# Eight-stage block on one core: dummy matmuls taken out of TensorE's queue, and sixteen of the value-output copies moved from ScalarE to VectorE

## The reference, cut to what is computed

```python
x = x + tanh(g_xattn[0]) * linear_attention(ctx, ctx, layernorm(x))      # stage 0
x = x + tanh(g_ffn[0])   * experts_top1(layernorm(x))                    # stage 1, 8 experts, GELU
x = x + tanh(g_xattn[1]) * normed_cross_attention(layernorm(x), ctx)     # stage 2
x = x + tanh(g_ffn[1])   * experts_top2_and_shared(layernorm(x))         # stage 3, 8 experts + 1, SiLU
x = x + tanh(g_xattn[2]) * causal_attention(layernorm(x), ctx, ctx)      # stage 4, 16 heads of 64
x = x + tanh(g_ffn[2])   * quantized_conv_mlp(layernorm(x))              # stage 5
x = x + tanh(g_xattn[3]) * attention_over_ctx_and_x(...)                 # stage 6, 16 heads
x = x + tanh(g_ffn[3])   * coupled_mlp(layernorm(x))                     # stage 7, 3 cycles
```

```python
x[t] += w1[t] * y1[t] + w2[t] * y2[t]       # "combine"
```

## Time and profile before

| | before |
|---|---|
| median of 3 runs | 2359.4 us (2356.04 to 2359.98) |
| the profiled execution | 2356.04 us |
| its span, first to last instruction | 2354.2 us |
| TensorE matmul busy | 2181.8 us, 93% of the span |
| VectorE busy | 1418.2 us, 60% |
| ScalarE busy | 988.6 us, 42% |
| GpSimd busy | 131.5 us, 6% |
| mean granted TensorE clock | 0.964 |

### The profile page before, as it was taken

The page is one execution under the profiler, slowest core; times in us unless marked ns, Lnnn a source line. Parts: engine busy times, 40 slices in busy tenths (PEclk is TensorE's granted clock), DMA queues, the critical chain, the costliest instruction groups (busy, mean ns, idle before and its releaser), DMA issues. The chain is left out here.

```text
span 2354.2 us, 33701 instructions
## 1 busy us (share of the span) xinstructions
PE 2181.8 (93%) x12946; PEld 1549.2 (66%) x12946; DVE 1418.2 (60%) x3011; ACT 988.6 (42%) x1829; POOL 131.5 (6%) x122
## 2 busy tenths in 40 slices
PE   7996999987999899797799999999999999999988
PEld 4874899444899778645566666666666666666643
DVE  5974111573344678787566666666666666666555
ACT  5222433431111422378444454444444445445345
POOL 1002011005122000000100000000000000000000
PEclk9996999988999999899899999999999999999999
DMA  3603897123699600200000000000000000000001
GB/s 115 171 1 110 278 326 274 55 76 108 200 326 320 209 1 1 77 1 1 11 1 1 1 1 1 1 1 1 1 1 1 1 1 1 1 1 1 1 0 36
DMA packets 109258, 159.73 MB, mean 68 GB/s; under 512 B 12555, under 2 KB 85165, under 8 KB 109101
## 3 DMA queue, kind: packets, MB, share of 16 engines
q1 hardware_dynamic: 101805, 134.80, 17.4%
q0 software_dynamic: 7296, 22.78, 3.0%
HBM read 127.64 MB, written 29.91 MB: 67 GB/s over the span
## 5 line engine op out<-in xcount | busy, mean ns | idle before, releaser
L595 PE MATMUL ps<-arena,w_odd 128*128 128x128 f32 (+4 forms) x2352 | 438.7, 440 | 3.1 <-DVE arena L1975 1.2
L595 PE MATMUL ps<-arena 128*64 128x256 f32 (+5 forms) x2852 | 411.0, 389 | 24.1 <-DVE arena L2058 7.5
L2272 DVE TENSOR_REDUCE small<-ps 128x1 f32<-128x1024 f32 x256 | 312.5, 1221 | 87.1 <-PE ps L595 87.1
L595 PEld LDWEIGHTS ps<-arena 128*64 128x64 f32 (+4 forms) x2852 | 266.9, 150 | 138.3 <-issue 31.3
L1590 ACT ACTIVATE arena<-ps 128x512 f32<-128x512 f32 x256 | 139.0, 595 | 453.0 <-PE ps L1090 452.9
L595 PEld LDWEIGHTS ps<-arena,w_odd 128*128 128x128 f32 (+3 forms) x2352 | 246.9, 188 | 106.5 <-issue 101.2
L1597 ACT ACTIVATE w_odd<-ps,small 128x1101 f32<-128x1101 f32 x256 | 302.5, 1182 | 10.2 <-DVE small L2273 8.5
L1090 PEld LDWEIGHTS ps<-ident,w_odd 128*128 128x128 f32 x2048 | 222.3, 140 | 121.2 <-issue 109.9
L1090 PE MATMUL ps<-ident,w_odd 128*128 128x128 f32 x2048 | 281.0, 277 | 9.8 <-DVE arena L2213 3.1
L2290 DVE COPY arena<-ps 128x512 f32<-128x512 f32 x256 | 164.3, 682 | 4.3 <-PE ps L1090 2.0
L595 PE MATMUL ps<-xn_feat,w_even 128*128 128x512 f32 (+1 forms) x352 | 138.5, 525 | 2.8 <-DVE xn_feat L1875 1.9
(11 more groups left out here) (360 smaller groups left out, 2855.9 us busy)
## 6 DMA issues: line engine op xcount, KB each, us to landing
w_odd<-in_s_w SPq DMA_DIRECT2D x32, 1024.0 KB, 6.9
w_odd<-in_s_wgu SPq DMA_DIRECT2D x30, 704.0 KB, 5.8
w_even<-in_s_w SPq DMA_DIRECT2D x15, 1024.0 KB, 7.2
arena<-expert_rows_in SPq DMA_DIRECT2D x62, 130.0 KB, 4.5
w_odd<-in_s_wd SPq DMA_DIRECT2D x30, 256.0 KB, 3.5
out_feat<-in_s_wgu SPq DMA_DIRECT2D x10, 704.0 KB, 5.6
expert_rows_in<-zero_row POOLq DMA_DIRECT2D x1, 5070.0 KB, 33.3
vo_rows<-w_odd SPq DMA_DIRECT2D x8, 616.0 KB
```

Source lines behind the costliest of these rows:

```text
L595: return pe.matmul(o, lhsT, rhs, start=start, stop=stop, **kw)
L2272: link(dve.tensor_reduce(m, s6_main[h], AX.X, ALU.max, negate=True))
```

## The change

Two things are edited. First, `keep_busy` and its calls are removed, 139 dummy matmuls in all (72 + 34 + 6 + 3 x 9). Second, of the 32 vo copies of stage 3's end the 16 with even u leave ScalarE. VectorE makes them, in a function `vo_copies4(g)` that `combine` calls after each of its four groups: after group g it copies the units 8g, 8g + 2, 8g + 4 and 8g + 6, each when its product is there. The counts of the semaphores follow: `mk_no` counts one mk copy per unit and one vo copy for every second, and `vo_copied` waits on `vo_sb` for an even unit and on `prep_sb` for an odd one.

```diff
--- before.py
+++ after.py
@@ -344,11 +344,14 @@
 
         def mk_no(u):
 
-            return KT + 8 + 2 * u + 1
+            return KT + 8 + u + 1 + u // 2
 
         def vo_copied(eng, u):
 
-            eng.wait_ge(prep_sb, KT + 8 + 2 * u + 2)
+            if u % 2 == 0:
+                eng.wait_ge(vo_sb, VT + 8 + u // 2 + 1)
+            else:
+                eng.wait_ge(prep_sb, KT + 8 + u + 1 + (u + 1) // 2)
 
         up_base = {1: 0, 3: E0 * NB if 1 in stages else 0}
         dn_base = {1: 0, 3: NT if 1 in stages else 0}
@@ -594,16 +597,9 @@
             def mm(o, lhsT, rhs, start=True, stop=True, **kw):
                 return pe.matmul(o, lhsT, rhs, start=start, stop=stop, **kw)
 
-            def keep_busy(bank, n):
-
-                for _ in range(n):
-                    mm(PS[:, bank, :], identb[:, :], identb[:, :].unsqueeze(1).broadcast_to([P, 4, P]))
-
             def layer_norm(s):
 
                 n, tr, half = ln_no[s], tr_no[s], half_no[s]
-                if s in (2, 3, 4):
-                    keep_busy(7, 9)
                 for g in range(4):
                     if g < 2:
                         pe.wait_ge(ln_xn, NT * xn_no[n] + 8 * g + 8)
@@ -878,7 +874,6 @@
                 pe.wait_ge(dn_add, NT)
                 expert_tiles(1)
                 context2()
-                keep_busy(0, 72)
 
             def stage3():
                 layer_norm(3)
@@ -921,7 +916,6 @@
                 pe.wait_ge(dn_add, dn_base[3] + NT)
                 expert_tiles(3)
                 context4()
-                keep_busy(0, 6)
 
             def context2():
 
@@ -961,7 +955,6 @@
                     if t < NT - 4:
                         pe.wait_ge(x2_x, t + 1)
                         rows_part(t + 4)
-                keep_busy(3, 34)
 
             def stage5():
                 def rows_turn(t):
@@ -1381,8 +1374,9 @@
                     h, kc = divmod(u, KD)
                     act.wait_ge(prep_mm, KT + 16 + u + 1)
                     act.activation(s4_mk[:, :, kc, h * C:(h + 1) * C], PS[:, u % 4, 0:B * C].rearrange("p (b c) -> p b c", b=B), ACT.Copy).then_inc(prep_sb, 1)
-                    act.wait_ge(vo_mm, B * H + u + 1)
-                    act.activation(vo_t[:, u // 8, u % 8], PS[0:C, 4 + u % 4, 0:D], ACT.Copy).then_inc(prep_sb, 1)
+                    if u % 2 == 1:
+                        act.wait_ge(vo_mm, B * H + u + 1)
+                        act.activation(vo_t[:, u // 8, u % 8], PS[0:C, 4 + u % 4, 0:D], ACT.Copy).then_inc(prep_sb, 1)
 
             def stage4():
                 layer_norm(4)
@@ -1765,6 +1759,12 @@
                 for n in range(1, 16, 2):
                     dve.wait_ge(prep_mm, KT + n + 1)
                     dve.tensor_copy(s4_vt[:, n // 2], PS[:, n % 8, 0:B * C]).then_inc(vo_sb, 1)
+
+            def vo_copies4(g):
+
+                for u in range(8 * g, 8 * g + 8, 2):
+                    dve.wait_ge(vo_mm, B * H + u + 1)
+                    dve.tensor_copy(vo_t[:, u // 8, u % 8], PS[0:C, 4 + u % 4, 0:D]).then_inc(vo_sb, 1)
 
             def attention(s, gate, fill=None):
                 a = at_no[s]
@@ -1993,7 +1993,7 @@
                             dve.wait_ge(per["md_mm", st], base["md_mm", st] + n + 1)
                             dve.tensor_copy(mx_y[st][v % 2][:, j], PS[:, 4 + n % 2, 0:D]).then_inc(per["md_sb", st], 1)
 
-            def combine(st, weights):
+            def combine(st, weights, then=None):
 
                 for g in range(4):
                     dve.wait_ge(yg_in[g], yg_base[st] + 16 * len(weights))
@@ -2004,6 +2004,8 @@
                         link(last)
                     for t in range(4 * g, 4 * g + 4):
                         last = dve.bn_stats(lnst[:, t, :], X[:, t, :])
+                    if then:
+                        then(g)
                 link(last)
 
             def stage1():
@@ -2077,7 +2079,7 @@
                             n += 1
                 expert_tiles(3)
                 vt_copies4()
-                combine(3, [rt1[0], rt1[1]])
+                combine(3, [rt1[0], rt1[1]], vo_copies4)
 
             def stage2():
                 layer_norm(2)
```

## The result

| | before | after |
|---|---|---|
| median | 2359.69 us (2356.04 to 2360.96, 4 runs) | 2374.01 us (2373.64 to 2377.6, 4 runs) |
| ratio | | 1.0066, 95% interval 1.0049 to 1.0084 |
| the profiled execution, its span | 2356.04, 2354.2 us | 2373.05, 2371.2 us |
| mean granted TensorE clock | 0.964 | 0.952 |

A forecast was written before the change was run, and what follows sets the result against it. At three stage seams the last engine binds, VectorE without slack at stages 3 and 4. Copies 13 us plus 1.3, 1.1 and 1.0 for stages 2 to 4 made 16.4 over before: 2375.5 us, range 2366 to 2383.

The forecast's parts named there:

- Sixteen copies enter VectorE's queue: Seam of stages 3 and 4: copies and round trips to TensorE lengthen VectorE's queue, 13 us (10.5 full clock, 17.3 half).
- T: End of a combine group on VectorE; third copy forecast to start at T + 1.25, fourth at T + 2.1, full clock.
- The floor of 5.6 us without waits: Seam of stages 3 and 4: sixteen copies at 0.35 us each with no round trip at all, 5.6 us.
- Rival one: Seam of stages 3 and 4: round trips vanish, copies only cost themselves; +8.7 us in all, 2368; chance 0.12.
- The clock in the bursts: Seam of stages 3 and 4: TensorE waits some 4 us between bursts, so some start at half clock; hence 13 us.
- Rival two: Seam of stages 3 and 4: cold bursts throughout, seam of 36 us or more; +22.7 us in all, 2382; chance 0.16.
- The six and the nine of the last seam: Seam of stages 3 and 4: removing dummies saves 0 at the meeting, since their queue arrives before VectorE anyway.
- Three layer norms: Stages 2, 3 and 4: without dummies TensorE's clock is cold before the transposes, costing 1.3, 1.3 and 1.0 us.
- The gate products: Stage 3: 64 products of 9 columns may lose their warm first part; +0.4 us, bounds 0 to 1.8.
- rival three: Layer norms of stages 2 to 4: transposes don't raise the clock, first matmuls at half; +25.9 us, 2385; chance 0.04.
- rival four: Seam of stages 3 and 4: VectorE waits for DMA between groups, copies free; +2.4 to +3.4 us; chance 0.04.
- The vo rows: Their write to DRAM ends about 13 us later; some 30 us of cover before attention uses them, cost nothing.

The follow-up runs named there:

- a2_changed: The changed kernel run again without an edit, on another chip, against the kernel before: 2374.58 us, ratio 1.0059.
- e9: Copies moved, all dummies kept but the six behind unit 31, 13 more in TensorE's wait at units 4, 12, 20, 28; against the kernel before: 2369.78 us, 1.0041.
- e3: The changed kernel with two copies of each group before its statistics and two behind, against the kernel before: 2365.79 us, ratio 1.0034.
- e8: Copies moved, two before and two after each group's statistics, all dummies kept but the six behind unit 31; against the kernel before: 2366.98 us, 1.0019.
- e5: Copies moved, all dummies kept but the six behind unit 31, against the kernel before (2367.81 us on that chip): 2379.13 us, ratio 1.0047.
- e1: Only the sixteen copies moved to VectorE, all 139 dummies kept, against the kernel before: 2374.0 us, ratio 1.0066.
- e11: Kernel before with 14 and 28 dummies in stage 3's two routing waits and 31 instead of 34 at stage 2's end: 2356.11 us, ratio 0.9985.
- e2: The kernel before with only its 139 dummies removed, all vo copies on ScalarE: 2362.58 us, ratio 1.0012.
- e6: Kernel before with more dummies at stage 1's and 7's layer norms and stage 3's routing waits, 31 instead of 34 at stage 2's end: 2359.47 us, 0.9961.
- e7: The kernel before without the 72 dummies of stage 1's end and the 9 of stage 2's layer norm: 2368.26 us, ratio 1.0000.

## Why the prediction came out as it did

Forecast 2375.5, measured 2374.01; slower, as given 0.96. The mechanism is the one forecast, but that the sum came within 1.5 us is in part luck. In the profiled run the last seam cost 3.3 us less than the 13 taken; stage 3 behind the gate (2.2) and the end of the span (1.6), at which nothing was put, made up for it. In a2_changed the seam came to 12.5 and stage 3 ran 1.5 us faster than before, with nearly the same total. By its own steps:

**Sixteen copies enter VectorE's queue (13 us, 10.5 at full clock to 17.3 at half).** Right in mechanism, and each part seen by itself: two copies at once, a round trip ahead of the third and fourth. Mis-sized: the third copy starts at T + 1.15 and the fourth at T + 1.84 (T = 794.28), not 1.25 and 2.1. The third is early because its matmul starts at T + 0.46 (794.74), not T + 0.62: no row stood behind the 0.2 us for semaphore and weight load, and it was too much. The fourth follows by 0.69 us and not 0.85, because I took the units' pace of 0.44 us from ScalarE's queue and TensorE is faster than that at full clock. A group costs 2.18 (e9), not 2.5. The seam costs 9.1 us at full clock (e9), 9.7 in the change, under the lower bound of 10.5, and 12.5 in a2_changed. At half clock the terms do not double as I had it: a2_changed's third group costs 3.3, not 4.1. The four copies by themselves take 1.3 us (e3), not 1.7. The floor of 5.6 us without waits was met by e8's 5.5. Rival one had that floor as its price; it needs another order of the queue to come true.

**The clock in the bursts ("some bursts will start at 1.2 GHz and some not").** Right: a2_changed and e5 had bursts that began at half clock, the change's profiled run only such as fell within the burst, and e9 shows the price with the dips taken out. Rival two's full price was not seen; of the changed kernel's two profiles a2_changed came nearest, 31.6 us of the 36 that would have shown it.

**The six and the nine of the last seam ("elsewhere 0").** This step holds for the dummies in the kernel before only. Once the copies are moved, the six cost 2.7 us (a wait of 3.42 in e1 against 0.68 in e5), and taking them out is a gain. So by the traces the two edits do not add. The times fit that but do not show it: by the ratios the copies alone cost 15.6 us, the dummies' removal alone 2.8 and both 15.6, each give or take 2.5 to 4. I had summed them as if they did; the sum came near because I never priced the copies with the dummies in place.

**Three layer norms (1.3, 1.3, 1.0).** Measured 1.75, 1.33, 1.23 in the profiled run and 0.8, 0.8, 1.4 in a2_changed; 0.5 of the 0.6 us at the seam of 2 and 3 came back. The price of 1.3 came from one profile's stage 1, whose length without dummies varies from 7.90 to 8.57. The gate products cost 0.3 (0.4 forecast), but in a2_changed they gained 2.0, outside the bounds of 0 to 1.8 that I had set. The 1.4 us in the wide matmuls of stage 3 were not forecast and are scatter; e11 shows that this stretch is worth dummies of its own.

**Transposes and the clock (rival three).** Fell. In the change TensorE idled 19.62 us, ran nothing but stage 2's transposes from 431.76 on, and the clock had risen when the scores began at 439.17 (0.50 until 437.4, 1.00 from 438 on). Against the Trainium skill ("TensorE: Matmul & The Clock Gate", Part 4: PE-mode transpose), these fp32 transposes did bring the full clock.

**Combine waits for its rows (rival four, given 0.04 in one place and 0.03 in another).** Fell: no wait for DMA stands ahead of L2003 in any group at this seam.

**The vo rows.** Their cover held: attention's first use of them at 860.86, 15.55 us later than before, shows no wait.

## What to carry to other kernels

Work moved off an engine that nobody waits for, into the one queue that comes last at a meeting, cost its full length here (5.5 us), and its round trips on top (3.6 more at full clock); if it must stand there, put other work of that queue between the copy that frees a bank and the copy that needs the bank's next product. Dummy matmuls pay where the path goes through TensorE after a wait and the dummies end before the wait does; the same dummies behind the last product of a stage become a delay as soon as TensorE is the one who comes last. Two edits at one meeting point must be priced together, since which engine is last decides what each is worth.

## What the runs showed of the hardware

**The same program lands on different clocks.** Two profiles of the changed kernel, 2373.05 and 2372.30 us long, have seams of 28.8 and 31.6 us and gate products of 12.5 and 10.2 us. e2 spread over 10.5 us (2356.5 to 2367.0), its slow runs at the lower clock, where the kernel before, on that chip, spread over 7.2 in 18 runs.

**A busy TensorE at half clock.** In rows 9 TensorE counts as busy all the time from 516 to 528 with nothing but 9-column products. The clock falls from 0.97 to 0.50 at 518 and stays there for the next 10 us; in a2_changed, too, it fell to 0.50 under them, at about 522. What in them does it was not tested.

**A stall with no releaser in the trace.** In stage 3, while GpSimd issues the writes of expert rows, the expert tiles of four profiles (e5, e6, e7 and e9) take 5 to 11 us longer than in the others. In e7 TensorE, ScalarE and VectorE are all idle from 581.4 to 586.6. The waits of TensorE there (who waited for whom: us, times, longest) name no releaser:

```profile
PE ps L595 <- issue: 8.0, 2, 7.3
```

On the chip of e5, e6 and e7 the kernel before too was 7 to 10 us slower than on the others, so a comparison within that chip should be touched less than a single profile (e7's is 11 us over before's, 10.5 of it in this stretch, which e7 leaves as it was). Its cause was not looked for.
